# Attention probabilities transposed by DMA instead of TensorE, in a four-stage transformer kernel on one core

## The chip, the cores and the metric

One core of a Trainium2 chip runs the whole program. The metric is the device time of one execution in microseconds. A core has TensorE (PE in the rows; PEld is its weight load), VectorE (DVE), ScalarE (ACT), GpSimd (POOL), and SyncE (SP), which here only issues transfers and waits.

## The reference

For 16 batches of 256 tokens with 256 features the reference does, in this order:

```
x += tanh(g) * LayerNorm(Wout(attention(LN(x), ctx)))   # 16 heads of 64, 256 context rows + 1 null key/value
x += tanh(g) * quantised_ffn(LN(x))                     # fp8-like grid, 1024 hidden
x += tanh(g) * (decayed scan over ctx, gathered + W_in) # boundaries from a mask
x += tanh(g) * mixture_of_experts(LN(x))                # 8 experts, top 2
```

The change touches the first line only. There, for each head, `sim = q k^T / 8`, `attn = softmax(sim)` over 257 keys, `out = attn v`. All of it is wanted to near fp32 accuracy, so the kernel multiplies fp16 high and low parts: three products, high*high, high*low and low*high.

## The kernel before

**Steps.** The outer loop runs over steps -1 to 17. In step `i.n` every engine carries three parts of three batches interleaved: PRE makes queries, keys and values of batch n+1, ATTN does the attention of batch n, and POST does output projection, feed-forward part, scan and routing of batch n-1. Step 0 has no POST and step 15 no PRE. The experts (71 tiles of 128 rows) follow from step 16 on. The steps 1 to 14 have all parts and are alike.

**Pairs.** Inside a step each engine runs its own fixed program over eight pairs of heads, `for j in range(PAIRS)`; the order is written out by hand, differently for each engine, and engines meet only at semaphores. An instruction that waits holds back all that stands behind it on its engine. Two heads of a pair share the steps below:

1. TensorE `scores(j)`: 12 matmuls into the PSUM banks `S[0]`, `S[1]` (L1275).
2. VectorE `maxima(j)`: row maxima of both banks (L1796), then `nm` (L1799); `null_arg(j)` (L1803).
3. ScalarE `exps(j)`: four Exp with row sums into `prob`, fp32 in SBUF (L956), then the null key's Exp (L960).
4. VectorE `divide(j)`: sum and reciprocal (L1815, L1816), the null probabilities (L1817), and head 0's `prob` times the reciprocal (L1823). ScalarE `norm(j)` does the same for head 1 (L965).
5. TensorE `prob_T(j)`: eight 128x128 fp32 transposes into the banks `T[0]`, `T[1]` (L1142). It stands one pair later in TensorE's order, right behind `scores(j+1)`.
6. ScalarE `prob_high(j)`: copies T to fp16 `pTh` (L949). VectorE `prob_low(j)`: T minus pTh to fp16 `pTl` (L1808). Both stand in the next pair; in VectorE's order `prob_low(j-1)` lies between `maxima(j)` and `null_arg(j)`, so before `divide(j)`.
7. TensorE `values(j)`: 12 matmuls into `O` (L1303), also in the next pair, behind `scores(j+1)` and a piece of PRE or POST.

For pair 7 the steps 5 to 7 stand at the end of its own step. TensorE fills between these with units of PRE and POST (`k_unit`, `q_unit`, `v_unit`, `w1_unit`, `wout_unit`, `win_unit`, ...) whose results ScalarE and VectorE bring to SBUF (`one` at L936 makes the high part, `low` at L1760 the low part); three PSUM banks `W` go round. In VectorE's program, pieces of POST and PRE stand in each pair at three places: before `divide(j)`, behind it, and at the end of the pair.

**SyncE.** In step i it waits for its source buffers, loads x and context of batch n+2, then the expert weights of two half-experts (`lst`, `gst`), then `xres`, and at the end it waits for the finished rows and split weights and writes them to DRAM. In step 15 it also starts to load split expert weights (`expert_in`).

Of the kernel before, what the change touches and what calls it, by code (L numbers as in the profile page):

```python
# [14 lines left out]
P = 128  # L15
# [163 lines left out]
def build(nc, x, ctx, lens, g_xattn, g_ffn, Wq, Wkv, null_kv, Wout, ln_scale, ln_bias, w1, b1, w2, b2,  # L179
          W_in, b_in, g_res, g_init, router_scale, router_w, gating_w, linear_w, expert_scale, out):  # L180
    es = ExitStack()
    with es:
# [100 lines left out]
        spare = sb("spare", [P, 6720])  # L283
# [57 lines left out]
        dech, decl = sb("dech", [P, 2, NTOK], FP16), sb("decl", [P, 2, NTOK], FP16)  # L341
# [90 lines left out]
        s_prob = [sem("prob_normed0"), sem("prob_normed1")]  # L432
        s_pT = [sem("probT0"), sem("probT1")]
        s_pTh = [sem("probT_high0"), sem("probT_high1")]
        s_pTl = [sem("probT_low0"), sem("probT_low1")]
# [90 lines left out]
        def _(sp):  # L526
# [34 lines left out]
            def rows_out(i, post, work):  # L561
                k, nfull, _ = work.at["win"][0]
                wait_apart(sp, free[k], nfull)
                sp.dma_start(pick(out_v, post.n), x3[:, :, :]).then_inc(s_x3o, 16)
                wait_apart(sp, s_nrm["ln4"], post.n + 1)
                sp.dma_start(pick(x4_v, post.n), x4[:, :, :]).then_inc(s_x4o, 16)

            def step(i, parts):
                work.begin(i.n, parts)
                post, nxt = i.shift(-1), i.shift(2)  # L570
                if i.n == 1:
                    sp.wait_ge(s_blank, 16 * TT * (NB - FIRST_BATCHES))
                if ATTN in parts and PRE in parts:
                    wait_apart(sp, s_nrm["ln1"], i.n + 1)
                    wait_apart(sp, s_u, i.n + 1)
                if PRE in parts and not (isinstance(i.n, int) and i.n + 2 >= NB):
                    sp.dma_start(xl[nxt.par][:, :, :], pick(x_v, nxt.n)).then_inc(s_x[nxt.par], 16)
                    sp.dma_start(cx[nxt.par][:, :, :], pick(ctx_v, nxt.n)).then_inc(s_c[nxt.par], 16)
                if ATTN in parts:
                    if i.n == 0:  # L580
                        sp.wait_ge(s_setup, 1)
                    else:
                        sp.wait_ge(s_lsp, i.n)
                    sp.dma_start(lst[:, :, :], pick(lin_v, i.n)).then_inc(s_lw, 16)
                    sp.dma_start(gst[:, :, :], pick(gat_v, i.n)).then_inc(s_gw, 16)
                    if POST in parts:
                        wait_apart(sp, s_xb, i.n)
                    sp.dma_start(xres[:, :, :], pick(x_v, i.n)).then_inc(s_xr, 16)
                if PRE not in parts and ATTN in parts:

                    sp.wait_ge(s_pv, PAIRS * i.n)
                    sp.wait_ge(s_go, 16 * i.n)
                    sp.wait_ge(s_lo, 16 * i.n)
                    for e in range(early):
                        expert_in(e)
                if POST in parts and ATTN not in parts:
                    sp.wait_ge(s_pv, PAIRS * NB)
                    sp.wait_ge(s_go, 16 * NB)
                    sp.wait_ge(s_lo, 16 * NB)
                    for e in range(early, E):  # L600
                        expert_in(e)
# [1546 lines left out]
```

## Time and profile before

| | |
|---|---|
| median of 3 runs | 1578.78 us (1574.91 to 1578.94) |
| the profiled execution | 1575.19 us, of which the span from first to last instruction is 1573.4 us |
| mean granted TensorE clock | 0.981 of full speed |
| busy TensorE, VectorE, ScalarE, GpSimd | 1455.4, 1200.8, 927.6, 635.8 us |
| attention steps 0 to 15 | from 68.5 us to about 1208 us of the span |
| one full step (steps 1 to 14 are alike) | 71.5 us |

Busy time of an engine is the union of its instructions' spans; matmuls overlap in their pipeline, so a group's busy time is more than what the engine would save without it. Idle time is put down to what ended it.

### The profile page before, as it was taken

The numbers are of one execution on the slowest core, as the hardware profiler recorded it, in microseconds if no ns is written. First come the engines' busy times: TensorE is split into PE (matmuls) and PEld (weight loads), VectorE is DVE, ScalarE is ACT, GpSimd is POOL, SyncE is SP. The second block draws the span as 40 slices with busy tenths as digits, with TensorE's granted clock in tenths as the row PEclk, the third lists the DMA queues.
The fourth block names the chain that finished last, engine by engine and source line by source line (L and its number), as shares of the span: only waits on it lengthen the run. The fifth ranks groups of instructions, "written<-read, shape, count | busy, mean of one in ns | idle before, by whom it ended". The sixth has DMA issues, their size and how long they took to land.

```text
span 1573.4 us, 36260 instructions
## 1 busy us (share of the span) xinstructions
PE 1455.4 (92%) x12542; PEld 1073.2 (68%) x12542; DVE 1200.8 (76%) x3275; ACT 927.6 (59%) x2530; POOL 635.8 (40%) x773
## 2 busy tenths in 40 slices
PE   2999999999999999999999999999967899999997
PEld 2667676767677776767677776767645666666665
DVE  6578888898989898888989898888875545454443
ACT  4476676767676767667676767767654432333332
POOL 6201333424342434424242424334234566555553
PEclk7999999999999999999999999999987999999999
DMA  8202020120202020211202020201232634333231
GB/s 265 86 1 69 10 74 22 61 75 9 81 2 82 2 81 15 69 49 34 82 2 81 2 82 8 75 23 41 73 109 91 188 65 64 57 61 53 50 61 22
DMA packets 78176, 93.44 MB, mean 59 GB/s; under 512 B 21312, under 2 KB 61776, under 8 KB 78000
## 3 DMA queue, kind: packets, MB, share of 16 engines
q1 hardware_dynamic: 51488, 73.21, 14.0%
q0 software_dynamic: 15680, 17.78, 6.9%
q8 instruction: 107, 1.75, 0.5%
q10 hardware_dynamic: 10832, 0.13, 0.4%
q14 instruction: 69, 0.57, 0.1%
HBM read 60.70 MB, written 31.30 MB: 58 GB/s over the span
## 4 chain that ended last, share of the span: by engine, by line
PE 52%; DVE 32%; ACT 9%; issue 4%; DMA 1%; POOL 1%; ACTq 0%; SPq 0%; POOLq 0%; DVEq 0%
PE S L1190 11%; PE W L1137 8%; PE W L1139 8%; PE W L1138 7%; DVE mx L1796 6%; PE O L1212 5%; PE T L1142 5%; ACT prob L956 4%; DVE pTl L1808 3%; PE O L1303 3%; PE S L1275 2%; PE W L1142 2%; DVE st_ln L1767 1%; DVE nm L1799 1%; ACT prob L965 1%
## 5 line engine op out<-in xcount | busy, mean ns | idle before, releaser
L956 ACT ACTIVATE prob<-S,nm 128x256 f32<-128x256 f32 x512 | 235.9, 475 | 88.0 <-DVE nm L1799 87.7
L753 POOL TENSOR_SCALAR ve_ln<-mv_ln 128x2 f32<-128x2 f32 x64 | 14.4, 225 | 534.5 <-DVE mv_ln L1770 534.5
L949 ACT ACTIVATE pTh<-T 128x512 f16<-128x512 f32 x256 | 139.4, 596 | 115.9 <-PE T L1142 107.9
L1808 DVE SCALAR_TENSOR_TENSOR pTl<-T,pTh 128x512 f16<-128x512 f32 x256 | 164.1, 680 | 9.9 <-ACT pTh L949 9.9
L1796 DVE TENSOR_REDUCE mx<-S 128x2 f32<-128x512 f32 x256 | 163.1, 678 | 9.1 <-PE S L1275 9.0
L1190 PE MATMUL S<-GL,xgh 128*128 x568 | 168.9, 379 | 0.1
L716 POOL DMA_INDIRECT out_dram<-ysb,tab x71 | 112.6, 1586 | 114.7 <-issue 67.0
L965 ACT ACTIVATE prob<-prob,rden 128x256 f32<-128x256 f32 x256 | 116.2, 501 | 71.3 <-DVE p0n L1817 71.3
L1142 PE MATMUL T<-ident,prob 128*128 128x128 f32 x1024 | 141.9, 283 | 0.4 <-DVE prob L1823 0.3
L1137 PE MATMUL W<-cTh,Wkh 128*128 128x256 f16 x512 | 140.5, 274 | 0.0
L1138 PE MATMUL W<-cTl,Wkh 128*128 128x256 f16 x512 | 140.5, 274 | 0.0
L1139 PE MATMUL W<-cTh,Wkl 128*128 128x256 f16 x512 | 140.4, 274 | 0.0
L905 ACT ACTIVATE gel<-S 128x512 f32<-128x512 f32 x71 | 42.4, 597 | 153.4 <-PE S L1190 140.5
L1142 PEld LDWEIGHTS T<-ident,prob 128*128 128x128 f32 x1024 | 113.1, 143 | 25.0 <-issue 23.0
L1707 DVE SCALAR_TENSOR_TENSOR xgl<-T,xgh 128x256 f16<-128x256 f32 x71 | 30.1, 425 | 118.9 <-ACT xgh L899 118.9
L1303 PE MATMUL O<-pTh,vh 128*64 128x256 f16 x512 | 76.5, 287 | 33.9 <-DVE pTl L1808 31.6
L1190 PE MATMUL S<-GL,xgl 128*128 x284 | 107.6, 379 | 0.0
L956 ACT ACTIVATION_READ_ACCUMULATOR prob<-S,nm 128x1 f32 x512 | 105.1, 205 | 0.0
L1212 PE MATMUL O<-GL,aH 128*128 x568 | 97.0, 273 | 4.6 <-DVE aL L1724 4.6
L1137 PE MATMUL W<-Wkh,cTh 128*128 128x512 f16 x256 | 97.3, 380 | 0.0
L1138 PE MATMUL W<-Wkl,cTh 128*128 128x512 f16 x256 | 97.0, 379 | 0.0
L1139 PE MATMUL W<-Wkh,cTl 128*128 128x512 f16 x256 | 97.0, 379 | 0.0
(311 smaller groups left out, 4364.3 us busy)
## 6 DMA issues: line engine op xcount, KB each, us to landing
cx<-in_ctx_dram SPq DMA_DIRECT2D x16, 512.0 KB, 5.3
gst<-in_L_ffn_gating_w_dram SPq DMA_DIRECT2D x16, 512.0 KB, 6.2
gating_split<-gsp SPq DMA_DIRECT2D x16, 512.0 KB, 2.7
GL<-gating_split SPq DMA_DIRECT2D x8, 1024.0 KB, 5.2
stg<-in_L_xattn_Wkv_dram SPq DMA_DIRECT2D x8, 512.0 KB, 13.5
xl<-in_x_dram SPq DMA_DIRECT2D x16, 256.0 KB, 4.2
lst<-in_L_ffn_linear_w_dram SPq DMA_DIRECT2D x16, 256.0 KB, 5.2
xres<-in_x_dram SPq DMA_DIRECT2D x16, 256.0 KB, 2.7
```

The source lines that it names most:

```text
L949: A(flat(pTh[:, h, :, :]), T[h][:, :], ACT.Copy).then_inc(s_pTh[h], 1)
L956: ins = A(prob[:, h, t, :], S[h][:, t * NTOK:(t + 1) * NTOK], ACT.Exp, bias=nm[:, h, t:t + 1], scale=SM, accum_out=rs[:, h, t:t + 1])
L965: ins = A(prob[:, 1, t, :], prob[:, 1, t, :], ACT.Copy, scale=rden[:, 1, t:t + 1])
L1137: M(o, lh, rh, start=start, stop=False)
L1138: M(o, lh, rl, start=False, stop=False)
L1139: return M(o, ll, rh, start=False, stop=stop)
L1142: return nc.tensor.transpose(o, src, ident[0:n, 0:n])
L1190: ins = M(o[:, :], (xgl if n == 2 else xgh)[i % 2][:, k, :], GLflat[:, bass.ds(w, HID)], start=(k == 0 and n == 0), stop=(k == KD - 1 and ...
L1212: ins = M(Y[:, 0:D], (aL if n == 2 else aH)[:, c * P:(c + 1) * P], GLflat[:, bass.ds(w, D)], start=(c == 0 and n == 0), stop=(c == 3 and n ...
L1303: ins = M(O[h * DH:(h + 1) * DH, c], lhs, rhs, start=(kt == 0 and n == 0), stop=(kt == 1 and n == 2))
L1796: ins = V.tensor_reduce(mx[:, h, :], S[h][:, :].rearrange("p (t k) -> p t k", t=TT), AX.X, ALU.max)
L1808: V.scalar_tensor_tensor(flat(pTl[:, h, :, :]), T[h][:, :], 1.0, flat(pTh[:, h, :, :]), ALU.mult, ALU.subtract).then_inc(s_pTl[h], 1)
```

## The change

The transposes leave TensorE. ScalarE's `norm` now multiplies both heads by the reciprocal and writes fp16 `ph`; VectorE's `prob_low` now computes `prob * rden - ph` from SBUF into fp16 `pl`, in quarters of 128x256, in the pair's own step; VectorE no longer scales head 0. SyncE then issues four transposing transfers for each pair, SBUF to SBUF, 128x512 fp16 each: high of both heads, then low of both heads. `pTh` and `pTl` are double-buffered by pair; `values(j)` waits for all four. `exps(j+1)` waits for `pl(j)`, since `prob` is single. SyncE's other transfers are spread over its eight pairs. In places the order of ScalarE and VectorE changes: x1T's copies go ahead of `norm(2)` and `prob_low(2)`, and two of the four `relus` ahead of `norm(3)`. To find room, five buffers share homes with others (`sq`, `x2`, `xhTh/xhTl`, `dech`, `decl`).

```diff
@@ sync
+            def probs_T(g, h, src, ready, dst, done):
+                sp.wait_ge(ready[h], g + 1)
+                at_least(sp, s_pv, g - 1)
+                sp.dma_start_transpose(dst[g % 2][:, h, :, :, :].rearrange("p t k r -> p (t k) r"),
+                                       src[:, h, :, :].rearrange("p t k -> p (t k)")).then_inc(done[g % 2], 16)
...
+                for j in range(PAIRS):
+                    if j == 0 and i.n > 0:
+                        gating_out(i.n - 1, gates_of[i.n - 1])
+                    if j == 1:
+                        if i.n > 0:
+                            linear_out(i.n - 1)
+                        if i.n > 1:
+                            x4_out(post.shift(-1))
+                    if j == 2:
...
+                        sp.dma_start(lst[:, :, :], pick(lin_v, i.n)).then_inc(s_lw, 16)
...
+                    if j == 3 and loads:
+                        sp.wait_ge(s_u, i.n + 1)
+                        sp.dma_start(cx[nxt.par][:, :, :], pick(ctx_v, nxt.n)).then_inc(s_c[nxt.par], 16)
+                    if j == 4:
+                        sp.dma_start(gst[:, :, :], pick(gat_v, i.n)).then_inc(s_gw, 16)
+                    if j == 5:
...
+                        sp.dma_start(xres[:, :, :], pick(x_v, i.n)).then_inc(s_xr, 16)
+                    if not pre and j in (3, 5, 6):
...
+                        expert_in((3, 5, 6).index(j))
+                    if j == PAIRS - 1 and post_:
+                        x3_out(post)
+                    for h in range(2):
+                        probs_T(g, h, ph, s_ph, pTh, s_pTh)
+                    for h in range(2):
+                        probs_T(g, h, pl, s_pl, pTl, s_pTl)
@@ scalar
-                def prob_high(j):
...
                 def exps(j):
-                        at_least(act, s_pT[h], i.n * 8 + j)
+                        at_least(act, s_pl[h], i.n * 8 + j)
                 def norm(j):
+                    g = i.n * PAIRS + j
+                    act.wait_ge(s_rden, g + 1)
+                    at_least(act, s_pTh[(g - 1) % 2], 32 * ((g - 1) // 2 + 1))
+                    for h in range(2):
+                        for t in range(TT):
+                            ins = A(ph[:, h, t, :], prob[:, h, t, :], ACT.Copy, scale=rden[:, h, t:t + 1])
+                        ins.then_inc(s_ph[h], 1)
@@ tensor
-                def prob_T(j):
...
                 def values(j):
-                    for h in range(2):
-                        pe.wait_ge(s_pTl[h], i.n * 8 + j + 1)
+                    g = i.n * PAIRS + j
+                    pe.wait_ge(s_pTh[g % 2], 32 * (g // 2 + 1))
+                    pe.wait_ge(s_pTl[g % 2], 32 * (g // 2 + 1))
@@ vector
                 def prob_low(j):
+                    g = i.n * PAIRS + j
+                    at_least(dve, s_pTl[(g - 1) % 2], 32 * ((g - 1) // 2 + 1))
                     for h in range(2):
-                        dve.wait_ge(s_pTh[h], i.n * 8 + j + 1)
-                        V.scalar_tensor_tensor(flat(pTl[:, h, :, :]), T[h][:, :], 1.0, flat(pTh[:, h, :, :]),
-                                               ALU.mult, ALU.subtract).then_inc(s_pTl[h], 1)
+                        dve.wait_ge(s_ph[h], g + 1)
+                        for t in range(TT):
+                            ins = V.scalar_tensor_tensor(pl[:, h, t, :], prob[:, h, t, :], rden[:, h, t:t + 1],
+                                                         ph[:, h, t, :], ALU.mult, ALU.subtract)
+                        ins.then_inc(s_pl[h], 1)
                 def divide(j):
-                    for t in range(TT):
-                        ins = V.tensor_scalar(prob[:, 0, t, :], prob[:, 0, t, :], rden[:, 0, t:t + 1], None, ALU.mult)
-                    ins.then_inc(s_prob[0], 1)
@@ vector, order of a step
                     if attn:
                         maxima(j)
-                        if j:
-                            prob_low(j - 1)
                         null_arg(j)
...
-                    if j == 3 and post_:
-                        boundaries()
+                    if j == 3:
+                        if attn:
+                            prob_low(j)
+                        if post_:
+                            boundaries()
                     if j == 4:
                         if pre:
                             k_low(2)
                         if attn:
+                            prob_low(j)
                             attn_low(1)
```

Behind `divide(j)`, VectorE has this to do before `prob_low(j)`: in pair 0 the two ctxT lows and the rows of `normed("ln1")`; in 1 `k_low` and `add_residual`; in 2 `k_low` and x1T's low; in 3 nothing; in 4 `k_low`; in 5 `k_low` and `decayed`; in 6 nothing; in 7 `fourth_norm`. The rest of each pair's pieces stands behind it.

## Rows read from the trace of the kernel before

**Rows 1.** The page: busy times, and the chain that ended last by engine.
```profile
PE 1455.4 (92%) x12542; PEld 1073.2 (68%) x12542; DVE 1200.8 (76%) x3275; ACT 927.6 (59%) x2530; POOL 635.8 (40%) x773
PE 52%; DVE 32%; ACT 9%; issue 4%; DMA 1%; POOL 1%; ACTq 0%; SPq 0%; POOLq 0%; DVEq 0%
```
**Rows 2.** Busy time in one full step: stretch length, engines, clock, DMA share.
```profile
630.37:701.87 71.50, 68.89 (x650) 52.30 (x647) 62.61 (x183) 49.85 (x143) 26.43 (x37) 1.00 0.14 46
```
**Rows 3.** TensorE timeline, pair 5 of step 7: start, length, line, count.
```profile
601.80 1.09 PE L1142 MATMUL T<-ident,prob 128*128 128x128 f32 x8
602.73 0.27 PE L1137 MATMUL W<-cTh,Wkh 128*128 128x256 f16 x1
```
**Rows 4.** Waits in that full step: us in total, times, longest.
```profile
DVE bnd L1871 <- PE W L1397: 2.8, 1, 2.8
...
DVE den L1815 <- ACT p L960: 2.1, 4, 0.8
...
DVE vl L1760 <- ACT vh L936: 0.9, 1, 0.9
...
DVE aTl L1786 <- ACT aTh L940: 0.7, 2, 0.3
```
**Rows 5.** VectorE timeline, pair 3 of step 8, idle time in brackets.
```profile
657.86 1.28 DVE L1796 TENSOR_REDUCE mx<-S 128x2 f32<-128x512 f32 x2
659.40 1.28 DVE L1808 SCALAR_TENSOR_TENSOR pTl<-T,pTh 128x512 f16<-128x512 f32 x2
660.60 0.15 DVE L1803 TENSOR_TENSOR d<-nm,ns 128x4 f32<-128x4 f32 x1
661.58 0.16 DVE L1815 TENSOR_TENSOR den<-rs,p 128x4 f32<-128x4 f32 x1 [0.83 <-ACT p L960]
662.07 0.74 DVE L1823 TENSOR_SCALAR prob<-prob,rden 128x256 f32<-128x256 f32 x2
```
**Rows 6.** ScalarE timeline, the same pair.
```profile
659.51 0.47 ACT L956 ACTIVATE prob<-S,nm 128x256 f32<-128x256 f32 x1 [0.27 <-DVE nm L1799]
662.20 0.91 ACT L965 ACTIVATE prob<-prob,rden 128x256 f32<-128x256 f32 x2 [0.66 <-DVE p0n L1817]
663.01 3.23 ACT L988 ACTIVATE hq<-W,b1c 128x256 fp8e4<-128x256 f32 x8
```
**Rows 7.** VectorE timeline, pieces of pairs 1, 2, 5 and 6 of step 8.
```profile
643.33 0.86 DVE L1838 SCALAR_TENSOR_TENSOR x<-W,mv_lno,sc_b 128x256 f32<-128x256 f32 x2
645.19 0.61 DVE L1823 TENSOR_SCALAR prob<-prob,rden 128x256 f32<-128x256 f32 x2
645.72 0.68 DVE L1760 SCALAR_TENSOR_TENSOR kl<-W,kh 128x512 f16<-128x512 f32 x1
646.32 0.87 DVE L1849 SCALAR_TENSOR_TENSOR x<-x,rstd_lno,xb 128x256 f32<-128x256 f32 x2
...
652.01 0.73 DVE L1777 TENSOR_SCALAR xh<-x,mv_ln,rstd_ln 128x256 f32<-128x256 f32 x2
...
677.52 0.75 DVE L1767 BATCH_NORM_STATS2 st_ln<-x 128x6 f32<-128x256 f32 x2
...
685.46 0.68 DVE L1760 SCALAR_TENSOR_TENSOR xhTl<-W,xhTh 128x512 f16<-128x512 f32 x1
```
**Rows 8.** SyncE timeline, step 8: issues of transfers.
```profile
631.38 0.33 SPq L607 DMA_DIRECT2D gating_split<-gsp  x1
631.75 1.21 SPq L610 DMA_DIRECT2D linear_split<-lsp  x1
```
**Rows 9.** DMA queues: packets, MB, share of 16 engines' span; then issues: KB, us to landing.
```profile
q1 hardware_dynamic: 51488, 73.21, 14.0%
q10 hardware_dynamic: 10832, 0.13, 0.4%
xres<-in_x_dram SPq DMA_DIRECT2D x16, 256.0 KB, 2.7
GL<-gating_split SPq DMA_DIRECT2D x8, 1024.0 KB, 5.2
```

More of the change, by code:

```diff
@@ L570, in step @@
                 post, nxt = i.shift(-1), i.shift(2)
+                pre, attn, post_ = PRE in parts, ATTN in parts, POST in parts
+                loads = pre and i.n + 2 < NB
+                if attn:
+                    gates_of[i.n] = work.at["gT"]
                 if i.n == 1:
                     sp.wait_ge(s_blank, 16 * TT * (NB - FIRST_BATCHES))
-                if ATTN in parts and PRE in parts:
-                    wait_apart(sp, s_nrm["ln1"], i.n + 1)
-                    wait_apart(sp, s_u, i.n + 1)
@@ L576, in step @@
[L576 to L601, printed above, removed]
@@ L602, in step @@
[L602 to L611 removed]
+                if not attn:
+                    if i.n == NB:
+                        gating_out(NB - 1, gates_of[NB - 1])
+                        linear_out(NB - 1)
+                        x4_out(post.shift(-1))
+                        sp.wait_ge(s_pv, PAIRS * NB)
+                        sp.wait_ge(s_go, 16 * NB)
+                        sp.wait_ge(s_lo, 16 * NB)
+                        for e in range(early, E):
+                            expert_in(e)
+                        x3_out(post)
+                        x4_out(post)
+                    if loads:
+                        sp.dma_start(xl[nxt.par][:, :, :], pick(x_v, nxt.n)).then_inc(s_x[nxt.par], 16)
+                        sp.dma_start(cx[nxt.par][:, :, :], pick(ctx_v, nxt.n)).then_inc(s_c[nxt.par], 16)
+                    return
@@ L981, in v_high, with relus @@
                     one("v", m, vh[nxt.par][:, m // 2, (m % 2) * 512:(m % 2 + 1) * 512], 1 / WS)
-                def relus():
-                    for m in range(4):
+                def relus(units=(0, 1, 2, 3)):
+                    for m in units:
                         k, nfull, _ = work.at["w1"][m]
@@ L2064, in step @@
                             pick_boundaries()
[L2065 to L2066 removed]
+                    if j == 3:
+                        if attn:
+                            prob_low(j)
+                        if post_:
+                            boundaries()
                     if j == 4:
```

130 lines of the change are left out of this document (67 added, 63 removed).

## The prediction

> **What bounds the kernel now.** I read the page first. TensorE is busy for 92% of the span and holds 52% of the chain that ended last, VectorE 32% [rows 1]: a chain that changes hands, so TensorE is the bound by a small margin at most. Next the busy time of one full step, since 14 steps repeat to within 0.1 us: of 71.5 us TensorE is busy for 68.9 and idle for 2.6, VectorE is busy for 62.6 [rows 2]. VectorE has 8.9 us of slack, and the waits of the step say what it is made of: 2.8 for TensorE's count of boundaries, 2.1 for ScalarE's exponentials, 0.9 and 0.7 for high parts [rows 4]; the rest is gaps of dependent instructions and smaller waits. Only the 2.8 is TensorE's lateness. So TensorE, relieved, could come down by no more than some 3 us before VectorE's own order sets the step, unless VectorE is relieved too. That is what the sum below turns on.
>
> **TensorE.** Eight transposes start at 601.80 and the next unit at 602.73 [rows 3]: 0.93 us for each pair, 7.4 a step. Its busy time falls to 61.5, and with today's 2.6 us of idle time it could do a step in 64.1. Nothing is added to it but waits. The removed copies out of T are ScalarE's and VectorE's.
>
> **ScalarE.** It loses two copies of 128x512 and gains two more pieces of `norm` (0.91 for two, 0.40 apart [rows 6]). Busy 49.9 of 71.5 [rows 2], it stays about the same; cost nothing by itself, but its place in the chain matters below.
>
> **VectorE's work.** Out go head 0's scaling, 645.19 to 645.72, 0.53 [rows 7], and the two pTl, 659.40 to 660.60, 1.20 [rows 5]: 1.73 a pair, 13.8 a step. In come four quarters of `prob * rden - ph`, each 128x256 from SBUF with a per-row scalar. The nearest row is the residual's same form, 0.87 for two, about 0.39 from start to start [rows 7]: 1.56 a pair, 12.5 a step. (Bounds: the plain scaling's 0.26 below, if the form ran at that rate, 8.3 a step; 0.6 for a 512-wide piece above, which would be 19.) So VectorE saves only 1.3 us of work a step.
>
> **VectorE's waits, the term that decides.** Today `prob_low(j-1)` fills the time in which ScalarE makes the exponentials of pair j. In pair 3 maxima start at 657.86, the next work at 660.60 and `den` at 661.58, after 0.83 of waiting [rows 5]. Without the 1.20 of pTl, VectorE is free about 1.6 after the start of maxima, and `den` cannot start before 3.6 to 3.7: a window of 2.0 that only the pieces ahead of `divide` fill. Pair 0 fills it (null part, routing, statistics, 2.9). Pair 1 has attn_out_scaled and xT's low, 1.4; pair 2 the norm, 0.7; pairs 3 and 4 nothing; 5 and 7 a residual of 0.75 and statistics of 0.95 (one of each shown), 1.7; pair 6 xhT's low, 0.6 [rows 7]. Waits: 0.6 + 1.3 + 2.0 + 2.0 + 0.3 + 1.4 + 0.3 = 7.9 a step, against 2.1 now.
>
> A second wait is new. `prob_low(j)` needs `ph(j)` of the same pair. `norm` starts 0.62 behind `den` and needs 0.91 for one head (661.58, 662.20 [rows 5, 6]), so ph is there 1.55 behind `den`; VectorE is free 0.49 behind it (662.07). It waits 1.1 less what stands between: nothing in pair 6 (1.1), k_low in 4 (0.5), a norm in 7 (0.4), enough in 0, 1 and 5, nearly enough in 2 (0.1). In pair 3 two relus units, four activations of 0.40 [rows 6], go ahead of `norm`, so it starts some 1.0 later: 2.1. Together 4.2. Between the heads VectorE's 0.78 meets ScalarE's 0.81: nothing.
>
> Sum for a step: 71.5, less today's waits 2.8 + 2.1 + 0.9 + 0.7 = 65.0; less 13.8 is 51.2; plus 12.5 is 63.7; plus 7.9 and 4.2 is 75.8. Some waits of 0.2 to 0.3 for scores and pTh, 0.8 together, go as well: 75.0. These waits are latencies of a ping-pong (maxima, exp, divide, norm, low), so they don't shrink when TensorE is earlier, and `exps(j+1)` may not start before `pl(j)`, which VectorE has done before maxima(j+1) anyhow. The step grows by 3.5, and TensorE, at 64.1, gets 11 us of idle time. I take 3.5; the bounds are 70.8 (75.0 less 4.2, for quarters at 0.26) and 77.5 (if GpSimd's use of SBUF slows the new SBUF reads by a fifth).
>
> **The transfers.** The trace has no transposing one and none from SBUF to SBUF, so I bound them. SyncE's issues took 0.33 to 1.21 us [rows 8]; four a pair are 1.3 to 4.8, in a pair of 9.3. I take 0.5. For the moving time: q1's packets took 14.0% of 16 engines' span [rows 9], 3524 engine-us for 73.21 MB and 51488 packets, so 0.39 us for 128 KB if bytes count, and 68 ns a packet of 1.4 KB. If a transpose moves rows of 128 fp16 values, 256 bytes, it has 512 of them: 2.2 us if each costs as much as a mean packet. q10's packets of 12 bytes took 9 ns; between the two a 256-byte one would take 20 ns, so 0.62 us a transfer. I take 0.6, since the row nearest in size is q10's. Landing of 256 KB took 2.7 from issue [rows 9]. The low part of head 1 then lands some 3.5 us behind `pl`, with a little queue.
>
> Who waits for that: `values(j)`, and behind it all of TensorE's later units. In pairs 0 to 6 VectorE still has 1 to 2.3 us of work in the pair when pl is ready, and in the next pair TensorE has 3 to 5 us to do between `values` and the end of `scores` of the pair after, in a pair of 8 to 9.4: 5.5 us of landing are hidden. Pair 7 is tighter. pl(7) is ready 6.7 behind its maxima, the next step's maxima come at 12.4, and values, rank and scores need 1.9: 3.8 are hidden. So 3.5 costs nothing; each us beyond costs a us a step, and beyond 5.5 up to one a pair. SyncE's queue: its loads are 9 a step at 0.5, the waits for `ph(j)` come in order and the loads queued behind them are wanted a pair or more later; `gating_out`, 512 KB, lands well before ph(0). Double-buffered pTh and the shared homes add waits on work that is long done (x4 written out a pair before `second_norm`). I cost them at nothing; the cover is one pair, 8 us.
>
> The Trainium skill (DMA: Bandwidth & Descriptors, Latency and other measured facts) gives a DMA transpose 261 GB/s when the middle dimension isn't contiguous, which would be 0.5 us for 128 KB; no row here shows one. It would leave my sum as it is.
>
> **Ends.** Step 0 is made of shorter pairs (no POST), in which the ping-pong's least length of 6.7 us bites more: I put 5 us. In step 15 the weights of three experts are loaded ahead of the transposes of pairs 3, 5 and 6, each 1.5 MB (1 MB lands in 5.2 [rows 9]), so these transfers land 5 us later; VectorE's table work covers some: 8 us. The experts' stage doesn't change. Sum: 14 x 3.5 + 5 + 8 = 62. The profiled execution took 1575.2, 3.6 under the median of the three; 1575.2 + 62 = 1637.
>
> **Rivals.**
> (a) The transfers are the bound. At 2.2 us each, four are 8.8 a pair, 70.4 a step, and with today's 14% of 71.5, 10.0, that is 80.4; latency behind a full queue is then 8 to 10 us instead of 3.5, which TensorE doesn't hide: 82 to 90 a step, 1575 + 16 x 10.5 to 18.5 = 1743 to 1871. For it: nothing but the bound from mean packets, and an issue of 1.21. It begins to count at 1.0 us a transfer. The Trainium skill (VectorE: DVE Perf Modes, The three transpose paths) gives 1309 ns to one 128x128 block by DMA against 390 ns on TensorE; if the four blocks of a transfer did not overlap, that would be 5.2 us a transfer, 168 us a step, some 3100 us in all. No row here shows it, and I think the blocks overlap. Chance 0.25.
> (b) Faster: VectorE's quarters run like the plain scaling, at 0.26 from start to start, and TensorE's relief counts. This is one mechanism, in `prob_low`: 12.5 becomes 8.3, the step 70.8; and if the ping-pong's waits are then half as long as I think, 65 to 67 near TensorE's own 64.1. It wins from below 0.28 for a quarter: 1575 + 13 - 14 x 0.7 = 1578 at first, and 1575 + 5 - 14 x 5.5 = 1503 with short waits; middle 1545. For it: TensorE's 92%. Against it: the residual's row and the window in rows 5, which isn't work but latency. Chance 0.18.
> (c) All cancels, 1571 to 1580: chance 0.07. That the change isn't what it says I hold for nothing: the diff removes every transpose of prob from TensorE.
> The forecast itself has 0.50, own range 1600 to 1690.
>
> A difference of 0.3% (4.7 us) is about what a measurement of this kernel tells from none. Faster 0.18, within 0.07, slower 0.75 (0.50 + 0.25). The range goes from 1550, into (b), to 1800, into (a).
>
> **What would show it.** A step from scores(0) to scores(0) of 75 us, TensorE idle for 11 of it; VectorE busy for about 61, waiting for `p` (L960's kind) 8 us and for ph 4 us; the quarters 0.39 apart; transfers landing within 4 us, so that TensorE's values wait little. If values wait long for a transfer and SyncE or the queues are full, it is (a). If VectorE's idle time has not grown, the prediction's main step is wrong.

## The result, and the profile after

| | before | after |
|---|---|---|
| median of the runs on one chip | 1576.9 us (1574.1 to 1578.9) | 1751.7 us (1745.3 to 1753.6) |
| profiled execution, span | 1575.2, 1573.4 | 1751.7, 1749.9 |
| from maxima(0) of step 1 to maxima(0) of step 15, a step | 71.6 | 82.5 (78.7 to 85.3) |

The ratio is 1.110 [1.107, 1.114]: 175 us slower where 62 were forecast. Of the span's 176.5, 14 steps of 11.0 are 153.6, the stretch ahead of them has 11.5 and that behind them 11.4. All medians here are of runs in the chip's usual, faster state; one of e12's four runs was in the slower one and is left out. The page of the kernel after answers to [rows 1, 9]: busy times, the queue (packets, MB, share of 16 engines), and the chain that ended last.

```profile
PE 1420.5 (81%) x11518; PEld 1009.3 (58%) x11518; DVE 1236.5 (71%) x3275; ACT 886.9 (51%) x2530; POOL 641.5 (37%) x773
...
q1 hardware_dynamic: 330016, 140.38, 34.3%
...
DVE 30%; PE 29%; ACT 16%; SPq 10%; DMA 9%; issue 5%; POOL 0%; ACTq 0%; POOLq 0%; DVEq 0%
```

VectorE did not get lighter: 1200.8 us before, 1236.5 now. SyncE's queue and the transfers have entered the chain with 19%. Waits of the kernel after in step 9, its shortest (us, times, longest), against [rows 4]:

```profile
PEld O L1334 <- issue: 13.0, 7, 3.6
PE O L1334 <- DMA pTl<-pl: 12.4, 7, 3.3
...
DVE den L1845 <- ACT p L997: 6.9, 6, 1.9
...
DVE pl L1837 <- ACT ph L1005: 3.2, 3, 1.7
```

VectorE's waits came nearly as forecast (7.9 and 4.2 forecast, 6.9 and 3.2 measured). TensorE's, 12.4 for the last low part, did not: I had them hidden. SyncE's issues for pair 4 of that step show why (start, length, count; the first row also holds a wait for head 1's `ph`), then VectorE's quarters of that pair and TensorE's `values`, and from the page the time from issue to landing:

```profile
850.50 3.15 SPq L570 DMA_TRANSPOSE pTh<-ph  x2
853.74 2.54 SPq L570 DMA_TRANSPOSE pTl<-pl  x2
856.33 0.57 SPq L642 DMA_DIRECT2D xres<-in_x_dram  x1
```

```profile
850.59 1.67 DVE L1837 SCALAR_TENSOR_TENSOR pl<-prob,rden,ph 128x256 f16<-128x256 f32 x4 [0.46 <-ACT ph L1005]
857.63 0.43 PE L1334 MATMUL O<-pTh,vh 128*64 128x256 f16 x2 [3.33 <-DMA pTl<-pl]
```

```profile
pTh<-ph SPq DMA_TRANSPOSE x256, 2.5
pTl<-pl SPq DMA_TRANSPOSE x256, 2.4
```

One issue takes 1.25 us and four stand in a row behind each other. Here `pl` is ready at 852.26 and `values` starts 5.4 us later, when the last low part has landed; over all pairs the median from `pl` to its landing is 4.6. Moving is cheap, as forecast: q1's share less 12.6% for its other loads is 0.217 x 16 x 1750 / 512 = 11.9 us of one DMA engine a transfer, 0.74 if all 16 share it, and 22 ns for each of its 544 packets (forecast 20). The Trainium skill (VectorE: DVE Perf Modes, The three transpose paths) gives 1309 ns for one block of 128x128 by DMA; the measured landing of four blocks in 2.4 us decides against adding them up.

Now the same steps pair by pair: length, then busy time of PE, PEld, DVE, ACT, POOL, granted clock, DMA share. First the kernel before, pairs 0 to 7 of step 8:

```profile
632.10:640.60 8.50, 8.50 (x84) 7.44 (x83) 8.06 (x36) 6.10 (x19) 2.30 (x4) 1.00 0.88 283
640.60:649.34 8.74, 7.84 (x80) 6.37 (x79) 8.57 (x25) 5.55 (x17) 4.44 (x8) 1.00 0.08 27
...
657.86:666.69 8.83, 8.31 (x85) 6.65 (x84) 5.05 (x14) 7.04 (x21) 7.39 (x8) 1.00 0.01 1
666.69:674.08 7.39, 7.39 (x78) 6.09 (x77) 6.12 (x17) 5.06 (x16) 5.36 (x6) 1.00 0.02 2
674.08:682.80 8.72, 8.67 (x75) 5.90 (x74) 8.55 (x22) 6.47 (x18) 4.00 (x6) 1.00 0.01 2
682.80:689.99 7.19, 7.15 (x63) 4.57 (x62) 5.64 (x16) 4.67 (x15) 0.57 (x1) 1.00 0.00 1
689.99:703.62 13.63, 12.75 (x107) 8.52 (x108) 12.81 (x42) 8.72 (x23) 2.35 (x6) 1.00 0.12 40
```

Then the kernel after, step 9:

```profile
806.85:816.92 10.07, 10.07 (x86) 8.80 (x87) 9.63 (x36) 6.91 (x21) 2.30 (x4) 0.89 0.16 33
816.92:826.52 9.60, 8.06 (x83) 6.53 (x82) 8.87 (x26) 5.30 (x16) 4.70 (x8) 1.00 0.47 114
...
835.68:844.37 8.69, 7.11 (x75) 5.66 (x74) 4.88 (x14) 6.53 (x21) 7.31 (x7) 1.00 0.44 113
844.37:853.44 9.07, 7.55 (x79) 6.08 (x77) 6.74 (x16) 4.70 (x15) 5.67 (x7) 1.00 0.51 114
853.44:863.78 10.34, 6.90 (x48) 3.79 (x47) 9.55 (x23) 5.21 (x16) 4.83 (x6) 0.83 0.50 102
...
sum 78.66, PE 64.16 PEld 47.46 DVE 64.82 ACT 47.06 POOL 27.16; mean PE 8.02 PEld 5.93 DVE 8.10 ACT 5.88 POOL 3.39
```

This is the table that I should have made before predicting. In pair 0 of the kernel before VectorE is busy 8.06 of 8.50, in pair 1 8.57 of 8.74, in pair 5 8.55 of 8.72: these three pairs left VectorE hardly any room, though the step as a whole gave it 8.9 us of slack. (TensorE's row is full in pair 0 too, so the table alone doesn't say whose pair it is; e14 below does.) In pair 0 the kernel after has 9.63 of 10.07: the same 0.44 idle, and the whole growth of the pair is VectorE's work. In pair 1 its work grows by only 0.30 and its idle time by 0.56, in pair 5 by 1.00 and 0.62. VectorE's timeline in pair 0, in pair 4 (`nm`) and in pair 5, and what GpSimd does beside `nm` and beside the quarters of pair 5 (L873 and L874 write `dech` and `decl`, which share the buffers that the profile names `onehot` and `cum`):

```profile
813.24 1.23 DVE L1803 TENSOR_SCALAR xn<-xl,mv_ln,rstd_ln 128x256 f32<-128x256 f32 x2
814.39 1.66 DVE L1837 SCALAR_TENSOR_TENSOR pl<-prob,rden,ph 128x256 f16<-128x256 f32 x4
...
845.67 1.03 DVE L1825 SCALAR_TENSOR_TENSOR nm<-mx,ns 128x4 f32<-128x4 f32 x1
...
859.22 3.39 DVE L1837 SCALAR_TENSOR_TENSOR pl<-prob,rden,ph 128x256 f16<-128x256 f32 x4
```

```profile
845.52 1.16 POOL L855 TENSOR_TENSOR lsp<-lst,lsp 128x512 f16<-128x512 f32 x1
...
859.84 0.80 POOL L873 CAST onehot<-dec 128x512 f16<-128x512 f32 x1
860.72 1.21 POOL L874 TENSOR_TENSOR cum<-dec,onehot 128x512 f16<-128x512 f32 x1
```

The quarters take 1.66, beside GpSimd's operations 3.39. The norm ahead of them in pair 0 takes 1.23 and took 0.72 before, `nm` in pair 4 1.03 and took 0.53. The contention is not new: in the kernel before it fell on pair 5's norm (1.43 against 0.73 in pair 2 [rows 7]), which now is free of it. It has moved, and grown. The small operations show its form: `nm` ends at 846.70 and GpSimd's `lsp` at 846.68, and in the whole trace each of the 31 operations on 128x4 there (`nm` and `den`) that took over 0.38 us ends 14 to 19 ns behind one of GpSimd's, in 29 cases a `TENSOR_TENSOR`. These were held until GpSimd's was over. The Trainium skill (GPSIMD Engine Reference, Specifications) says that GpSimd shares its SBUF interfaces with VectorE and contends with instructions that have two SBUF inputs; the quarters have two (`prob`, `ph`), what they replace had one (`pTh`) and took `T` from PSUM. The trace agrees: 3.39 against 1.66.

### The profile page after: what moved, and what is told of

It reads as the page before. It is cut to its first block, busy times and chain, and to the rows that moved or that the text cites. A ratio compares the mean times of both kernels' runs of the same rounds, so it can differ in the third digit from the quotient of the medians.

```text
span 1749.9 us, 34958 instructions
## 1 busy us (share of the span) xinstructions
PE 1420.5 (81%) x11518; PEld 1009.3 (58%) x11518; DVE 1236.5 (71%) x3275; ACT 886.9 (51%) x2530; POOL 641.5 (37%) x773
## 4 chain that ended last, share of the span: by engine, by line
DVE 30%; PE 29%; ACT 16%; SPq 10%; DMA 9%; issue 5%; POOL 0%; ACTq 0%; POOLq 0%; DVEq 0%
SPq L570 9%; PE S L1230 9%; ACT prob L993 8%; DVE pl L1837 7%; DMA pTl<-pl 7%; DVE mx L1822 7%; PE O L1252 4%; ACT ph L1005 3%; PE O L1334 3%; PE T L1182 2%; PE W L1177 2%; PE W L1178 2%; PE W L1179 2%; PE W L1420 2%; DMA out_dram<-ysb,tab 2%
## 5 line engine op out<-in xcount | busy, mean ns | idle before, releaser
L1837 DVE SCALAR_TENSOR_TENSOR pl<-prob,rden,ph 128x256 f16<-128x256 f32 x512 | 236.2, 522 | 62.3 <-ACT ph L1005 60.8
L1334 PE MATMUL O<-pTh,vh 128*64 128x256 f16 x512 | 85.3, 313 | 212.5 <-DMA pTl<-pl 212.3
L1005 ACT ACTIVATE ph<-prob,rden 128x256 f16<-128x256 f32 x512 | 218.7, 506 | 42.1 <-DVE p0n L1847 37.4
L1334 PEld LDWEIGHTS O<-pTh,vh 128*64 128x64 f16 x512 | 37.0, 118 | 251.6 <-issue 226.6
L1845 DVE TENSOR_TENSOR den<-rs,p 128x4 f32<-128x4 f32 x128 | 25.4, 198 | 122.6 <-ACT p L997 120.9
L1177 PE MATMUL W<-Wkh,cTh 128*128 128x512 f16 x256 | 103.8, 405 | 0.0
L1178 PE MATMUL W<-Wkl,cTh 128*128 128x512 f16 x256 | 102.8, 402 | 0.0
L1179 PE MATMUL W<-Wkh,cTl 128*128 128x512 f16 x256 | 102.7, 401 | 0.0
L841 POOL TENSOR_SCALAR onehot<-tokcol,bcur 128x256 f16<-128x256 f32 x32 | 29.6, 927 | 174.4 <-DVE bcur L1989 174.4
```

The costliest lines, as they stand in the source:

```text
L1005: ins = A(ph[:, h, t, :], prob[:, h, t, :], ACT.Copy, scale=rden[:, h, t:t + 1])
L1177: M(o, lh, rh, start=start, stop=False)
L1178: M(o, lh, rl, start=False, stop=False)
L1179: return M(o, ll, rh, start=False, stop=stop)
L1334: ins = M(O[h * DH:(h + 1) * DH, c].rearrange("d (t r) -> d t r", r=P), lhs, rhs, start=(kt == 0 and n == 0), stop=(kt == 1 and n == 2))
L1837: ins = V.scalar_tensor_tensor(pl[:, h, t, :], prob[:, h, t, :], rden[:, h, t:t + 1], ph[:, h, t, :], ALU.mult, ALU.subtract)
```

## Experiments

Medians on the chip; "a step" is the mean of steps 1 to 14, and pairs are means of steps 2 to 14. Before: 71.6 a step, pairs 8.50, 8.75, 8.52, 8.83, 7.40, 8.72, 7.18, 13.63. After: 82.5, pairs 10.08, 9.62, 9.69, 8.74, 10.31, 10.56, 8.06, 15.51.

### What the transfers cost (e1 to e4)

e1 has no transfers and writes both parts straight into the tiles of the matmuls, not transposed:

```diff
-                        probs_T(g, h, pl, s_pl, pTl, s_pTl)
+                        sp.wait_ge(s_pl[h], g + 1)
-  A(ph[:, h, t, :], prob[:, h, t, :], ...)
+  A(flat(pTh[g % 2][:, h, t, :, :]), prob[:, h, t, :], ...)
```

> The changed kernel without its transfers: ScalarE and VectorE write ph and pl straight to the buffers that values(j) reads, so the blocks are not transposed (that part of the computation is left out); every other instruction, wait and order is kept. My theory: the order of VectorE and ScalarE alone makes a step of 75 us as the prediction worked out, and the transfers' lateness the rest up to the 82.5 measured: 1640 us (1620 to 1660), step 75. Rival (the new order alone is to blame, the transfers are hidden): about 1750. Rival (TensorE's relief counts as soon as nothing lands late): under 1576, step of 65 to 70.

e2 makes one transfer of both heads, 128x1024, of the two of each part:

```diff
-  dma_start_transpose(dst[g % 2][:, h, ...], src[:, h, :, :])   # 4 a pair
+  dma_start_transpose(dst[g % 2][:, :, ...], src[:, :, :, :])   # 2 a pair
```

> Two transposing transfers a pair in place of four, 128x1024 each: both heads' high part, then both heads' low part. The issue of one took SyncE 1.25 us in the changed kernel. If that is a fixed price of an issue, the low part is issued 1.8 us earlier and lands some 1.8 us earlier: 1680 to 1700 us. If it goes by the blocks that are transposed (so 2.5 us for one of double size), the high part now starts 0.8 us later and the low one lands 0.7 us later than with four: 1760 to 1800.

e3 puts useless matmuls into TensorE's idle time (its edit is shown), e4 makes the four transfers plain copies:

```diff
+  for _ in range(12): M(T[1][:, 0:NTOK], before[:, :], Woh[:, 0, :], ...)
   pe.wait_ge(s_pTh[g % 2], 32 * (g // 2 + 1))
```

> The changed kernel with twelve matmuls of no use (128x256, to a PSUM bank that attention leaves free) put ahead of the wait of values(j), 1.3 us of work on TensorE in time in which it mostly waits. Theory that the half-clock stretches (two of 3.4 us a step, granted clock 0.92 against 0.98) cost the 3.8 us between the shortest step of 78.7 and the mean of 82.5: the clock rises to 0.97 and more and the time falls to 1700 to 1720. Rival, that the clock costs nothing because TensorE has idle time: 1750, or up to 1780 for the added work.

> The four transposing transfers are plain copies of the same bytes between the same buffers (blocks not transposed, that part is left out). Theory that the transposing issue's 1.25 us is what is late: issues of 0.4 us, low part landed 3 us behind pl instead of 4.7, time near the kernel without transfers, 1640 to 1660. Rival, that moving 67 MB more between SBUF buffers disturbs the engines whoever moves it: stays above 1700.

Measured: e1 1702.1 us (1.081 [1.078, 1.084]), e2 1711.8 (1.087 [1.085, 1.090]), e3 1740.6 (1.106 [1.101, 1.111]), e4 1708.4 (1.086 [1.083, 1.088]). The transfers thus cost 49 of 175 us, and two issues instead of four give 40 of these back, plain copies 43. The issue has one price at both sizes that were run; here a 128x1024 of e2, and two copies of e4:

```profile
788.32 1.24 SPq L571 DMA_TRANSPOSE pTh<-ph  x1
```

```profile
791.67 1.27 SPq L570 DMA_DIRECT2D pTh<-ph  x2
```

1.24 for 256 KB against 1.25 for 128 KB, and 0.63 for a copy. And 126 us remain with no transfer at all: the larger part of the loss lies in the work and order of the engines. e3 came out between its two theories; what it says of the clock stands below.

### The alternation, put off or removed (e5, e7, e8, e9)

e5 is e1 with a second `prob` and the low quarters of pair j-1 behind `maxima(j)`, where the kernel before had its low parts; e7 is the same with two real transfers and `values` later on TensorE (for room, `pTh` and `pTl` have one buffer each, and a few copies move behind it); e8 is e7 with `values` and these copies in their old places, ahead of the units that would hide the landing:

```diff
                         maxima(j)
+                        if j:
+                            prob_low(j - 1)
                         null_arg(j)
```

> The kernel without transfers once more (blocks not transposed, that part is left out), with one thing changed: prob has two buffers, and VectorE makes the low part of pair j-1 behind the maxima of pair j, as the kernel before did, instead of waiting for ph(j) in the pair itself. Theory: the ping-pong between VectorE and ScalarE makes the 78.4 us that the steps of the run without transfers share, and of that some 7 us are waits for the exponentials and 3 to 4 us for ph; both go, the step falls to about 69 (VectorE's work with little idle time), the time to 1540 to 1560, below the kernel before. Rival, that VectorE's work itself has grown (SBUF quarters, GpSimd beside it) and that the waits are no loss: stays at 1690 to 1700.

> The real thing in that order: high and low parts transposed by one transfer each (128x1024), low part made one pair later with two prob buffers, pTh and pTl with one buffer each to find the room, and values(j-1) moved behind TensorE's second piece of pair j, since the low part lands some 5.7 us behind the maxima. Theory: VectorE's order sets the step at 69 to 72 and the transfers are hidden: 1545 to 1590, at or a little below the kernel before. Rival, that TensorE waits for the low part again and the values' lateness comes back through attn_high: step of 75 to 78, 1620 to 1670.

> As the run before it, but values(j-1) stays where the changed kernel has it, ahead of TensorE's second piece. Theory: the low part lands 5.7 us behind the maxima, while values stands 3 to 4 us behind them, so TensorE waits 2 us a pair, 12 to 16 a step, and has 6 of them free: step 77 to 80, 1650 to 1700, clearly slower than with values moved. Rival, that the place does not matter because VectorE is the bound: within 0.5% of the run with values moved.

Measured: e5 1681.0 (1.067 [1.065, 1.069]), e7 1752.9 (1.114 [1.111, 1.118]), e8 2164.9 (1.373 [1.369, 1.377]). My theory, that the alternation of VectorE and ScalarE is most of the loss, missed by 120 us and more. In e5, putting the quarters off restores pairs 0 and 5 (8.50, 8.55) but makes `values` late (TensorE waits 7.1 us a step for low parts), and pairs 1 and 7 grow to 10.1 and 16.4. e8 was expected at 1650 to 1700: TensorE waits 507 us in all for low parts there, 151 in e7, and is at 1.2 GHz for 45 us of steps of 110. e5, e7 and e8 change several things at once and price none of them. It is e9 that takes VectorE's two waits for ScalarE away and little else:

```diff
-  dve.wait_ge(s_ph[h], g + 1)          # and s_exp, s_p0 ahead of den
-  stt(pTl.., prob[:, h, t, :], rden.., pTh..)
+  stt(pTl.., gi_b[:, 0:NTOK], rden.., Woh[:, 0, 0:NTOK])
-  link(V.tensor_tensor(den, rs, p0, ALU.add))
+  link(V.tensor_tensor(den, ones16[:, 0:4], ones16[:, 4:8], ALU.add))
```

> The order and the work of the changed kernel without transfers (probabilities written straight to the matmuls' tiles, not transposed), and with VectorE's two waits for ScalarE of each pair taken away: the denominator is summed from constants and not from the sums of the exponentials, and the low quarters are made from a constant f32 and a constant fp16 tile of the same sizes and not from the probabilities and their high parts. So attention's values are wrong and only times are read. Theory (the alternation of VectorE and ScalarE is what the new order lost): the waits of 6.9 us for exponentials and 3.2 us for high parts in a step of the run without transfers go, steps of 79.3 us become 72 to 74, and the time is 1590 to 1625 us, against 1702 us there. Rival (VectorE's own work, its contention with GpSimd and TensorE's lateness set the step; the waits are only where slack shows): the time stays over 1680 us.

Measured: 1666.4 us (1.057 [1.055, 1.059]), 36 less than e1 where 77 to 112 were expected, and still 90 over before. Pairs 0, 1 and 5 are unmoved (10.08, 9.59, 10.42). In pair 0 VectorE works as before. In pair 1 of e1 `den` waited 0.52 and then took 0.48; without the wait it starts earlier and is held by GpSimd:

```profile
686.93 1.07 DVE L1848 TENSOR_TENSOR den<-ones 128x4 f32<-128x4 f16 x1
686.84 1.15 POOL L830 TENSOR_TENSOR ul<-u,uh 128x512 f16<-128x512 f32 x1
```

It ends 4.0 us behind the pair's start in both, so this pair says nothing on the wait's price. Pairs 3 and 4 fall by 1.4 and 0.8, and pairs 6 and 7 give 0.9 of it back; their time at 1.2 GHz rises from 6.0 to 8.6 us a step.

### The place of VectorE's work (e6, e13, e14, e15)

e6 narrows the last two of GpSimd's operations in pair 5 to 8 columns in e1; e15 narrows the low quarters of pairs 0, 1 and 5 in e1.

```diff
-  link(pool.tensor_copy(dech[:, :, :], dec[:, :, :]))      # e6, decl alike
+  link(pool.tensor_copy(dech[:, :, 0:8], dec[:, :, 0:8]))
+  w_ = 8 if j in (0, 1, 5) and i.n != 0 else NTOK            # e15
```

> The kernel without transfers, in which GpSimd makes only 8 of 256 columns of the decay's high and low parts (blocks not transposed, decay parts not made in full: both left out). In pair 5 these two GpSimd instructions lie beside VectorE's four quarters of the low part, which took 3.39 us in place of 1.67. Theory that the two engines hinder each other at SBUF: the four take 1.7 us, pair 5 falls from 10.46 to about 8.9 us, the time by 15 x 1.5, to 1680. Rival, that the quarters are slow there for another reason: 1702, pair 5 still 10.4.

> The kernel without transfers, with the low quarters of pairs 0, 1 and 5 cut to 8 of 256 columns (from the second step on), so that the low parts are left out there; those of the other pairs stay whole. Theory by place: pairs 0, 1 and 5 fall from 10.08, 9.59 and 10.46 us to 8.5 to 8.9, 8.5 to 9.0 and 8.4 to 9.0; 3.5 to 4.5 us a step, the time 1635 to 1655 us against 1702. Rival (they stand beside other waits, and TensorE or the clock sets the step): over 1680 us.

Measured: e6 1677.9 (1.065 [1.063, 1.067]), pair 5 from 10.46 to 9.21: the contention with these two operations is 1.25 us a step. e15 1668.1 (1.059 [1.057, 1.061]), pairs 0, 1, 5 at 9.04, 8.56, 9.56, that is 3.0 less; pairs 6 and 7 grow by 0.6 together (their time at 1.2 GHz from 6.0 to 7.8), so 34 us are won and not 47 to 67.

The clean test puts the same four useless quarters into the kernel before, in pair 3 (e13) or in pair 0 (e14):

```diff
+  for r in range(4):
+      at_least(dve, s_scr, i.n * 4 + r)
+      V.scalar_tensor_tensor(scr[:, 0, :], gi_b[:, 0:NTOK], gi_b[:, 0:1],
+                             Woh[:, 0, 0:NTOK], ALU.mult, ALU.subtract).then_inc(s_scr, 1)
```

> The kernel before with four useless VectorE quarters (128x256 f32 and fp16 in, fp16 out, about 0.42 us each and a short wait between them, 1.7 to 2.2 us in all) in pair 3 of each step, where VectorE is idle 3.8 us. Theory by place: nothing or little is lost, within 8 us of before. Rival (VectorE's total work counts, wherever it stands): +25 us or more (16 x 1.7).

> The same four useless quarters in pair 0 of each step (in the first step in pair 3), where VectorE is idle 0.4 us. Theory by place: pair 0 grows from 8.5 us by the whole of them, 1.6 to 2.2 us, and the time by 20 to 35 us. Rival (a later slack of the step takes it up, as TensorE sets the step): within 8 us of before.

Measured: e13 1579.1, 3.6 over before (1.002 [1.001, 1.003]); e14 1619.2, 43.7 over (1.028 [1.026, 1.030]). One edit, 2.0 us of VectorE a step, costs twelve times as much in pair 0 as in pair 3. In e14 it costs more than itself (27 us would be 14 times the 1.96 below), and more than the 20 to 35 expected. Pairs 0 and 1 of step 8, and of step 10:

```profile
654.73:665.19 10.46, 10.46 (x102) 9.18 (x101) 9.92 (x40) 6.71 (x20) 2.30 (x4) 1.00 0.77 252
665.19:675.17 9.98, 7.12 (x58) 5.04 (x57) 8.67 (x26) 4.61 (x14) 4.46 (x8) 0.83 0.00 0
```

```profile
804.63:815.09 10.46, 10.46 (x102) 9.17 (x101) 9.92 (x40) 6.71 (x20) 2.30 (x4) 1.00 0.74 252
815.09:823.84 8.75, 5.89 (x62) 4.62 (x61) 8.58 (x26) 4.94 (x15) 4.44 (x8) 1.00 0.01 2
```

Pair 0 is 1.96 longer in both. In step 8 the granted clock then falls to 1.2 GHz for one stretch of 3.4 us (0.83 in the mean of pair 1), behind 2.3 us in which TensorE waited for pTl, and the pair takes 1.23 more. Step 10 is the only one of steps 2 to 14 without such a stretch.

### The clock (e10, e12, e16)

e10 and e12 are e1 and e9 with the useless matmuls of e3, e16 is e1 with 36 of them in one place, TensorE's idle time at the end of pair 5:

```diff
                     if j == 6:
+                        for _ in range(36): M(T[1][:, 0:NTOK], before[:, :], Woh[:, 0, :], ...)
                         rows_T("xhT", xh, ...)
```

> The kernel without transfers of the first experiment (not transposed, so wrong values), with 12 useless 128x256 matmuls ahead of TensorE's wait for the probabilities of each pair, so that TensorE has less idle time before it. Theory (the alternation sets the step; half-clock stretches cost little): the granted clock of the steps rises to about 1 and the time stays within 15 us of 1702 us. Rival (the half-clock stretches after TensorE's idle time carry a good part of the 126 us): under 1670 us.

> The kernel without transfers and without VectorE's two waits for ScalarE (constants in place of what they wait for, so wrong values), with the 12 useless matmuls of 128x256 ahead of each wait for probabilities. Theory: with both the alternation and the half clock gone what is left is VectorE's own work of 61 to 64 us a step and TensorE's 64 plus the useless matmuls' 10.5 (12 x 8 x 0.109), which fill only its idle time: 1580 to 1620 us, within 15 us of the same kernel without useless matmuls. Rival (the clock carries it): at least 25 us under the same kernel without useless matmuls.

> The kernel without transfers, with 36 useless 128x256 matmuls (3.9 us at full clock) at the end of TensorE's pair 5, ahead of the transposes of the normalized rows, where it is idle up to 6.1 us. Clock theory: the half-clock stretches behind (5 to 6 us of pairs 6 and 7) go, and pairs 6 and 7 fall from 24.0 us together to 21 to 22; 1660 to 1680 us against 1702. Rival (pairs 6 and 7 are long for VectorE's and ScalarE's sake): within 10 us of 1702 us.

Measured: e10 1742.9 (1.105 [1.103, 1.107]), e12 1700.4 (1.077 [1.072, 1.081]), 41 and 34 us above the same kernels without: 12 matmuls in every pair are too many where TensorE is the bound (pairs 6 and 7 are 26.4 in e10, 23.1 in e1), so these two say nothing on the clock. Nor does e3: its 11 us are what is left of a gain (half clock, 1.2 GHz, from 12.9 to 3.2 us a step) when the same matmuls have been paid. e16: 1695.0 (1.074 [1.071, 1.076]), 7 under e1, as its rival said. Half clock falls from 10.2 to 5.5 us a step and pair 6 from 9.22 to 8.00, but in pair 7 half clock rises from 2.0 to 4.6 and the pair from 13.91 to 14.40: 7 us is a net too.

The clock's price can be read in e1 itself, where pairs 6 and 7 have the same work in every step. Step 8, step 9, and pair 6 of e16 and of the kernel after, step 9:

```profile
753.52:763.45 9.93, 9.93 (x65) 5.49 (x64) 5.59 (x15) 5.40 (x16) 0.00 (x0) 0.73 0.00 1
763.45:777.54 14.09, 12.19 (x89) 7.83 (x89) 11.98 (x40) 7.18 (x20) 2.35 (x6) 0.88 0.08 28
...
834.56:843.25 8.69, 8.69 (x65) 5.23 (x64) 5.60 (x16) 5.28 (x16) 0.00 (x0) 0.84 0.00 0
843.25:856.60 13.35, 11.07 (x91) 6.75 (x91) 11.70 (x40) 7.45 (x21) 2.34 (x6) 1.00 0.06 21
```

```profile
750.93:758.93 8.00, 8.00 (x67) 4.95 (x66) 5.51 (x15) 5.29 (x16) 0.00 (x0) 1.00 0.01 3
```

```profile
863.78:871.78 8.00, 8.00 (x67) 4.95 (x66) 5.51 (x16) 5.29 (x16) 0.00 (x0) 1.00 0.22 44
```

Pair 6 is full of TensorE's work and takes 8.00, 8.69 or 9.93 by the clock; pair 7 takes 13.35 to 13.70 at full clock. Against the means of 9.22 and 13.91 that is 1.4 to 1.8 us a step, an estimate of 20 to 25 of e1's 126 us. In the kernel after, the steps differ by 6.6 us, and the longer ones have more half clock (5.7 us in step 9, the shortest, 12.9 in the mean); but TensorE's waits for the transfers differ there too, and the two were not separated.

### A version for the slack that there is (e11, e17, e18)

e11 sends head 1 of every pair by transfers and leaves head 0 to TensorE. e17 does so only in pairs 2, 6 and 7; e18 has the empty list, which leaves the reordering of the change alone:

```diff
+BY_DMA = (2, 6, 7)                       # e18: ()
-                    for h in range(2):
-                        probs_T(g, h, ph, s_ph, pTh, s_pTh)
-                    for h in range(2):
-                        probs_T(g, h, pl, s_pl, pTl, s_pTl)
+                    if j in BY_DMA:
+                        probs_T(i.n, j, 1, ph, s_ph, pTh, s_pTh)
+                        probs_T(i.n, j, 1, pl, s_pl, pTl, s_pTl)
+                def prob_T(j):                                # tensor
+                    for h in range(1 if j in BY_DMA else 2):
...
```

> Only the second head of each pair is split in rows and transposed by two transfers of 128x512 (high, low); the first head is normalized by VectorE, transposed on TensorE and split from PSUM one pair later, as in the kernel before. Nothing is left out. VectorE's normalizing of the first head (0.61 us) covers ScalarE's high parts of the second (0.87 us), so the second wait of the alternation nearly goes; two issues of 1.25 us and a landing of some 2.4 us end about 5 us behind the low parts' start, well ahead of the values of the next pair. TensorE's work falls by 3.7 us a step to about 65. Theory (what the change lost was the alternation for two heads and four issues in a row): steps of 70 to 73 us, 1555 to 1600 us. Rival (any transfer whose end the values wait for costs, or VectorE's quarters cannot sit between the divide and the other work): over 1620 us.

> Only head 1 of pairs 2, 6 and 7 is split in rows and transposed by transfers of 128x512; all other heads are normalized, transposed on TensorE and split from PSUM as in the kernel before. Nothing is left out. VectorE has 0.7 us (pair 2), 1.5 us (pair 6) and slack in pair 7 for it; with one head by transfers pair 3 went from 8.83 to 7.89 us and pair 7 from 13.63 to 13.02, while pair 2 grew by 0.24. Theory by place: 8.5, 8.75, 8.75, 7.9, 7.5, 8.72, 7.2, 13.0 = 70.3 us a step, 1.2 under before: 1555 to 1570 us. Rival (the three transfers' lateness or the clock takes it back): 1577 us or more.

> The kernel of e17 with no pair by transfers: all heads are normalized, transposed on TensorE and split from PSUM as in the kernel before, in the changed kernel's order of everything else. Nothing is left out. Theory (the transposes taken off TensorE earn it): pair 3 goes back from 7.48 to 8.4 to 8.8 us and pair 7 from 13.1 to 13.6; steps of 71 to 71.8 us, 1565 to 1580 us. Rival (the reordering earns it): steps under 70.3 us, 1560 us or less.

Measured: e11 1627.8 us (1.033 [1.031, 1.035]), a miss (1555 to 1600 was expected): pairs 0, 1, 5 and 4 grew by 0.8, 0.6, 1.1 and 1.7, more than pairs 3 and 7 won (0.9, 0.5). e17 1548.6 us, 0.983 [0.981, 0.984] of before: **1.7% faster than the kernel before**, 27 us under it, 203 under the change as made, and 6 under the range expected. e18 1580.5 us (1.004 [1.003, 1.005]), at the upper edge of its range. So the reordering costs 6 us, and the three transferred heads earn 32. Pairs 3, 4 and 7 of step 8 in e17:

```profile
643.91:651.39 7.48, 7.27 (x76) 5.86 (x75) 4.46 (x13) 6.13 (x20) 6.10 (x7) 1.00 0.57 181
651.39:658.46 7.07, 7.07 (x75) 5.77 (x74) 6.21 (x17) 5.03 (x15) 6.72 (x7) 1.00 0.02 2
...
674.39:687.51 13.12, 11.98 (x99) 7.65 (x100) 12.36 (x42) 7.75 (x21) 2.35 (x6) 1.00 0.21 50
```

and in e18:

```profile
658.41:666.72 8.31, 8.31 (x86) 6.90 (x85) 5.49 (x15) 7.02 (x22) 6.93 (x7) 1.00 0.03 3
666.72:674.64 7.92, 7.09 (x75) 5.75 (x74) 6.65 (x17) 4.97 (x16) 5.82 (x7) 1.00 0.00 0
...
690.54:704.71 14.17, 12.90 (x107) 8.62 (x108) 12.76 (x41) 8.73 (x23) 2.35 (x6) 1.00 0.06 20
```

Pair 3 is full of TensorE work in e18 (8.31 of 8.31), and the four transposes of pair 2's head 1 (half of the 0.93 of [rows 3]) leave it in e17, while VectorE's work there falls from 5.49 to 4.46. That is 0.5 of the 0.8 won in pair 3; why pair 4 wins 0.9 was not taken apart. The granted clock of these rows stays at 2.4 GHz.

## Why the prediction was wrong

Three terms failed: VectorE's work, the transfers' lateness and the clock. By step, 3.5 us were forecast and 11.0 measured. Step 9 has 7.2 of these 11.0; the other 3.8, from 78.7 to the mean of 82.5, are later landings and half clock together.

**TensorE** (the number met by chance): 64.1 was 61.5 of work plus 2.6 of today's idle time. Its busy time was 64.16 in step 9 and 67.0 in the mean of the steps, above 61.5, for a part of it ran at half clock.

**VectorE's waits** (right in size): 7.9 and 4.2, measured 6.9 and 3.2. I called them the term that decides. e9 without them wins 36 us of 175, and part of that wait was taken over by GpSimd's hold in pair 1.

**VectorE's work** (failed): "VectorE saves only 1.3 us of work a step", so 61.3; it grew to 64.8 in step 9 and 65.3 in the mean. The sum of step 9 goes wrong by just this: 75.0 forecast, 78.7 measured, VectorE's idle time 13.7 against 13.8. (That match is partly luck: the two waits are 2.0 under the forecast, the other gaps 2.1 over.) From start to start the quarters take 14.4 a step, not 12.5: 1.7 of it on pair 5's, beside GpSimd, and 0.2 on the others, 0.40 apart instead of 0.39. GpSimd also costs 0.5 on pair 0's norm, 0.5 on pair 4's `nm`, 0.5 on two other small operations, less 0.9 that pair 5's norm and `dec` no longer pay. That is 2.5 of the 3.5; the rest was not taken apart. I had bounded GpSimd's part by a fifth of the quarters' time; it doubles them where it strikes.

**The step as a pool.** Summed by step, 13.8 going out and 12.5 coming in cancel. By pair they don't: the low part of pair 7 left the end of the step before, and the quarters of pair 0 came into a pair with 0.4 us to spare. Pairs 0, 1 and 5 grew by 1.6, 0.9 and 1.8, 4.3 of the 11.0 a step; in step 9, 2.9 of it is added work and 1.2 added idle time. That the place decides what work costs is shown by e13 and e14; the slack of 3.8 in pair 3 paid for none of it.

**The transfers' issue** (failed): 0.5 taken from bounds of 0.33 to 1.21, measured 1.25, four in a row. "So 3.5 costs nothing" became a landing 4.6 behind `pl` in the median, up to 6.0 in the mean of pair 3, and 49 us (e1). Step 0 and the end hold 14 of them, the steps 2.6 each, in pairs 2, 4 and 7. At both ends together 13 us were forecast and 23 measured.

**The moving** (right): 20 ns a packet, measured 22. Rival (a) named 1743 to 1871 us, which holds the time, but by a mechanism that isn't there: the queue is 34% full. The whole range of 1550 to 1800 holds it too, only because it was stretched into (a); the forecast's own 1600 to 1690 does not.

**The clock** (put at nothing, without a reason): half-clock stretches of 12.9 us a step, none before. They cost some 20 to 25 us in e1 by the rows above; in the kernel after their price is not separated from the transfers' lateness.

Open: pairs 6 and 7 of e1 are 2.3 us longer than before. The clock is 1.4 to 1.8 of it by the rows above; the rest was not taken apart. Nor was it tried to move GpSimd's two operations away from the quarters of pair 5 in the whole kernel.

## What to carry to other kernels

Before pricing a change of a loop, split its body where the engines meet and list idle time by engine for each piece: an engine with 12% of slack in the whole can have none in the pieces that get the new work. Relief of the engine that is busiest in the sum pays only in the pieces where it is the bound; take the cheap offload there and nowhere else (three heads of sixteen gained 1.7%, all sixteen lost 11%). And count the issues of transfers as serial work of the queue that issues them. A pair that gets a wait can cost twice: e14 paid 1.96 us for the work and 1.23 more for TensorE's clock behind the wait.

## What the runs showed of the hardware

- A transposing SBUF to SBUF transfer took SyncE 1.25 us to issue, with 128 or with 256 KB; a plain one 0.63. It landed 2.4 to 2.5 us behind the start of its issue and cost 22 ns for each of 544 packets, most of them of 256 bytes.
- Four `scalar_tensor_tensor` quarters with both tensors in SBUF took 1.66 us alone and 3.39 beside GpSimd's operations. A `nm` of 128x4 grew from 0.16 to 1.03, and ended 17 ns behind GpSimd's `TENSOR_TENSOR`. The 16 low parts of a step that VectorE read from PSUM before took 0.67 to 0.69 each, also beside GpSimd's operations.
- A stretch of 3.4 us at 1.2 GHz behind 2.3 us of TensorE's idle time made one pair 1.23 us longer; it came in 12 of steps 2 to 14 and not in step 10, with the same work (e14). In e1 a pair full of matmuls took 8.69 us at a mean clock of 0.84 and 9.93 at 0.73; in e16 it took 8.00 at full clock.
